# A graph layer's row gathers: GpSimd's gathers wait for the fetched rows, and for the sums eight groups back from group 8 on

## The reference

```python
h = maximum(layernorm(x), 0)
p1 = tanh(h @ pp_W1 + pp_b1) @ pp_W2 + pp_b2
inter = concatenate([p1[src], p1[dst]])          # per edge, 128 values
inter = ((inter @ pi_W1 + pi_b1) @ pi_W2 + pi_b2) @ pi_W3   # 64 x 8 per edge
i1 = einsum('ecb,eb->ec', inter, basis)
i1 = tanh(i1 @ ii_W1 + ii_b1) @ ii_W2 + ii_b2
out = x + segment_sum(i1, dst)
```

## Time and profile before

| | us |
|---|---|
| timed runs, median of 3 | 1991.06 |
| timed runs, lowest and highest | 1988.24, 1992.56 |
| profiled execution, its span | 2703.6 |
| TensorE matmuls busy in it | 1947.7 |
| VectorE busy | 1439.4 |
| ScalarE busy | 1089.0 |
| GpSimd busy | 1483.3 |

### The profile page before, as it was taken

One profiled execution on the slowest core, in us unless ns is written; L12 is line 12 of the kernel. 1 busy time (PEld: TensorE's weight loads), 2 busy tenths in 40 slices (PEclk: granted clock), 3 DMA queues, 4 the chain that ended last, 5 costly groups with the idle time before them and its releaser, 6 DMA issues.

```text
span 2703.6 us, 54970 instructions
## 1 busy us (share of the span) xinstructions
PE 1947.7 (72%) x20012; PEld 1270.4 (47%) x20012; DVE 1439.4 (53%) x1939; ACT 1089.0 (40%) x2419; POOL 1483.3 (55%) x1581
## 2 busy tenths in 40 slices
PE   4112987777777777777777777777777777787788
PEld 3101654444544544544445444455444444554556
DVE  4302875555555555555555555555555554555556
ACT  2211653434443343444444444444443343444344
POOL 4773025555655555665656566666655555555551
PEclk9555998888988888898988888988988788788889
DMA  4311222222221221222222222222222222222221
GB/s 86 80 28 31 58 46 43 44 45 42 50 49 39 48 47 41 51 50 43 50 46 45 49 49 45 49 48 45 50 46 45 44 46 43 44 44 42 42 42 45
DMA packets 261709, 127.00 MB, mean 47 GB/s; under 512 B 183561, under 2 KB 233720, under 8 KB 261448
## 3 DMA queue, kind: packets, MB, share of 16 engines
q1 hardware_dynamic: 209967, 74.11, 13.1%
q0 software_dynamic: 50048, 51.35, 10.4%
q10 hardware_dynamic: 1558, 0.15, 0.1%
HBM read 119.47 MB, written 6.00 MB: 46 GB/s over the span
## 4 chain that ended last, share of the span: by engine, by line
PE 66%; issue 19%; another core or an unknown queue 8%; ACT 5%; DVE 1%; DVEq 0%; ACTq 0%
PE bank L1337 34%; PE bank L1320 10%; PE bank L1344 7%; PE bank L1427 6%; PE spread_ps L1329 5%; PE bank L1304 3%; ACT tt_sb L702 2%; ACT st_sb L714 2%; PE bank L1352 0%; DVE o_sb L945 0%; PE spread_ps L1166 0%; ACT t_sb L705 0%; DVE acc_all L899 0%; DVE loc_bc L893 0%
## 5 line engine op out<-in xcount | busy, mean ns | idle before, releaser
L526 POOL DMA_INDIRECT u_rows<-u_tab,src_e x1436 | 1357.4, 945 | 1102.8 <-PE bank L1320 750.9
L1337 PE MATMUL bank<-o_sb,g_sb 128*64 128x256 f32 x6256 | 943.3, 453 | 153.2 <-issue 144.5
L945 DVE TENSOR_TENSOR o_sb<-st_sb,spread_ps 128x2048 f32<-128x2048 f32 x391 | 889.7, 2275 | 229.3 <-remote 111.3
L714 ACT ACTIVATE st_sb<-bank,s_bias 64x256 f32<-64x256 f32 x1564 | 733.1, 469 | 182.2 <-PE bank L1320 90.6
L1009 DVE TENSOR_TENSOR hot_t<-loc_bc,bank 126x512 bf16<-126x512 bf16 x391 | 268.4, 687 | 942.6 <-remote 615.3
L1337 PEld LDWEIGHTS bank<-o_sb,g_sb 128*64 128x64 f32 x6256 | 522.3, 162 | 434.7 <-issue 307.9
L702 ACT ACTIVATE tt_sb<-bank,z_bias 128x256 f32<-128x256 f32 x391 | 185.0, 473 | 706.1 <-PE bank L1337 364.4
L1344 PE MATMUL bank<-ident,tt_sb 128*128 128x128 f32 x782 | 183.3, 319 | 369.8 <-issue 211.1
L705 ACT COPY t_sb<-bank 128x256 f32<-128x256 f32 x391 | 146.1, 374 | 569.3 <-PE bank L1344 306.8
L1427 PEld LDWEIGHTS bank<-hot,t_sb 128*65 128x65 f32 x3128 | 224.4, 143 | 184.5 <-issue 182.1
L1427 PE MATMUL bank<-hot,t_sb 128*65 128x42 f32 x3128 | 274.5, 239 | 19.4 <-issue 18.6
(11 more groups left out here) (148 smaller groups left out, 361.9 us busy)
## 6 DMA issues: line engine op xcount, KB each, us to landing
loc_bc<-loc_tab SPq DMA_DIRECT2D x391, 126.0 KB
u_rows<-u_tab,src_e POOLq DMA_INDIRECT x1436
v_win<-v_tab SPq DMA_DIRECT2D x391, 15.8 KB
basis<-edge_attr SPq DMA_DIRECT2D x24, 256.0 KB
v_tab<-acc_all SPq DMA_DIRECT2D x6, 336.0 KB
basis<-u_tab,src_e POOLq DMA_INDIRECT x100
u_tab<-basis SPq DMA_DIRECT2D x6, 224.0 KB
x_sb<-x SPq DMA_DIRECT2D x1, 1120.0 KB
```

Of the source, the lines that this page charges most:

```text
L526: pool.indirect_dma_start(out=u_rows[:, g % UR, j, :] if g >= AHEAD else first_u[:, g - XG, j, :], out_offset=None, in_=u_tab[:, :], in_of ...
L714: last = nc.scalar.activation(tiles[h * D:(h + 1) * D, j], s_ps[part].rearrange("p (q a e) -> p q a e", q=2, a=TILES), ACT.Identity, bias= ...
L945: return nc.vector.tensor_tensor(o_sb[:, r, :, :].rearrange("p c (j e) -> p j c e", j=TILES), st_sb[:, r, :].rearrange("p (j e) -> p j e", ...
L1337: last = nc.tensor.matmul(z_ps[h * D:(h + 1) * D, 0:2 * P], g_sb[:, c, :], o_sb[:, r, c, 2 * h * P:(2 * h + 2) * P], start=(c == 0), stop= ...
```

## The change

It touches only the loop of GpSimd's gathers. One wait is added before it: the gathers of the u table start when the rows fetched from x have gone through tanh (`rows_tanh` at four). And the wait for the sums of group g-8, which stood from group 40 on, stands from group 8 on. Buffers, order, count and targets of the gathers stay.

```diff
@@ -514,13 +514,14 @@
             with pool.If(is_fast):
                 pool.wait_ge(u_stored, 32 * NC)
                 pool.wait_ge(ld[0], ld_count(0))
+                pool.wait_ge(rows_tanh, len(UNITS))
                 for g in range(XG, NG):
                     k = g // PIECE
                     if g == FULL:
                         pool.wait_ge(last_in, 32)
                     if g % PIECE == 0:
                         pool.wait_ge(ld[k % LD], ld_count(k))
-                    if g >= AHEAD + UR:
+                    if g >= UR:
                         pool.wait_ge(s_ready, g - UR + 1)
                     for j in range(TILES):
                         pool.indirect_dma_start(
```

## The result

The kernel after takes 2022.82 us (median of four runs, 2021.02 to 2023.33), the kernel before 1990.94 us. The ratio is 1.0153, with a 95% interval of 1.0141 to 1.0166: slower by 28 to 33 us. The prediction was 2018 us.

A forecast was written before the change was run, and what follows sets the result against it. GpSimd's issue of gathers was taken to bound the kernel from group 40 on. That group's start moves from T + 135 to T + 164, 29 us, less 1 us at the start: +27 us, 2018 us, range 1985 to 2032.

The forecast's parts named there:

- What bounds the kernel: GpSimd's issue of gathers sets the time from group 40 on, TensorE runs behind it; 68 + 1920 + 18 = 2006 us.
- The 18 us behind the last gather: End of the run: 16 us from the last group's transposes to the span's end, some 2 us for the landing.
- the delays of the start: Delays of 5 to 30 us early in the first profile, taken for a cost of recording and not counted on.
- The pace of 4.10 us: TensorE's own time per step, where no gathers run; claimed faster than GpSimd's 4.9 to 5.0 us per group.
- The sum: Group 40's start moves from T + 135 to T + 164 for any T over 97: 29 us, less 1 us; +27 us.
- T: End of the last tanh of the fetched rows, taken at about 100 to 125 us, upper bound 193.
- B: Time at which GpSimd begins group 40; before, the later of 232 us and T + 135; after, T + 164.
- The 3 us added for first steps not yet overlapped: An estimate within TensorE's time for group 32's sums in the kernel before: T + 1 + 32 x 4.10 + 3.
- Part (b): Group g waits for the sums of group g-8 from group 8 on, before from group 40; should cost nothing.
- part (a): The wait for rows_tanh at four before the first gather; gathers start at T, where before they began at 68.22.
- The rule on VectorE and GpSimd: GpSimd can't write gather descriptors during VectorE's two-port operations; by its ratio 132 gathers take some 820 us, not 164.
- The gathers' cost beside steps: What gathers add to TensorE's steps; bounds nothing or up to 2.3 us a step; at 0.7 the change costs 7 us.

The follow-up runs named there:

- the second look: The kernel before, unchanged, timed and profiled once more: ratio 1.001 (1.000 to 1.002), span 1991.4 us.
- (b) alone: The kernel before with only the wait for the sums of group g-8 moved to group 8 on, no wait for rows_tanh: 2017.15 us, ratio 1.0124.

## Why the prediction was right

**What bounds the kernel**: right, and from a profile in which GpSimd waited 750.9 us. The step that carried it was the sum that stands outside the profile's own pace: 1536 gathers x 1.25 us + 68 + 18 = 2006 us against 1991 measured. The distance of 1.25 us holds in normal runs (1.255 and 1.256 us on average from group 40 on), so the conclusion of "1.24 us or a little less" was slightly off. The 15 us over were not in the gathers, which take 9 us more than the 1920 of the sum, but in the start: the first u gather is at 42.72 in the second look and not at 68.22, 25.5 us earlier. The 18 us behind the last gather were 19.6 and 20.6 us; of the 2 us for the landing, the median measured is 2.8 us (2.3 to 4.7).

**That the delays of the start were not to be counted on**: right, shown by the second look at the kernel before. The reason given, a cost of recording, is only half supported: the second execution was profiled as well and has none of them. They belonged to that one execution; that recording as such makes them isn't borne out.

**The pace of 4.10 us**: right up to group 32. In the second look TensorE has group 32's sums by 204.6 us (their matmuls start at 203.89), 131.7 us after the first group's.

**The sum**: its size was right, the branch it took was not, and that its size was right is in part luck. I had T at 100 to 125 us and so let TensorE's group 32 set B before (T + 135). T, the end of the last tanh, is 71.5 us in the kernel after and 72.5 in the second look, below the 97 us from which that branch holds, and the start of the gathers lies at 42.72 and not at 68.22. The 3 us added for first steps not yet overlapped aren't seen either: TensorE has group 32's sums at T + 132, not T + 135. So GpSimd itself set B before, and the price is the plain difference of the first gathers: 72.28 - 42.72 = 29.6 us. B was 209.68 before and 238.46 after, 28.8 us apart, against the 29 predicted. Both branches gave the same number because TensorE has the sums of group 32 within 5 us of the time when GpSimd reaches group 40 (204.6 and 209.68). With T alone put right, the recorded sum would have given 232 against 72 + 164 = 236, a cost of 4 us. The two terms that were mis-sized, T by 30 to 50 us and the landing of u by 26 us, came from the first profile's late start, and their errors cancelled in the difference. The forecast of +27 us lies just under the measured 28 to 33. The two normal profiles are 27.8 us apart and the medians 31.9; no run here parts these 4 us from the scatter of single executions.

**Part (b) at no cost beside part (a)**: right; the kernel after waits 1.2 us in all for TensorE's sums (the line on L1321 in the fence below). Said of the pair, it hid that (b) alone would cost 26 us, which the prediction's own formula gives (T + 1 against the end of group 7's gathers).

**The rule on VectorE and GpSimd** of the page "SBUF — State Buffer" of the Trainium skill: the measurement decided against its price for this kernel. In the normal runs a gather takes a median 944 ns in the first hundred, nearly all of which lie beside VectorE's products in the kernel after, as the later ones do in the kernel before. The page's price is for two-port operations. The products here read one operand from SBUF and one from PSUM, and no run shows whether any VectorE operation in these steps is a two-port one, so the rule itself isn't tested. The summary lines of the kernel after and of the second look:

```profile
L527 POOL DMA_INDIRECT basis<-u_tab,src_e x100: 940/944/1453, 72.3 to 197.3; - x100
...
  PE bank L1321: 1.2, 4
```
```profile
L526 POOL DMA_INDIRECT basis<-u_tab,src_e x100: 940/944/1373, 42.7 to 167.8; - x100
```

**The gathers' cost beside steps**, left between nothing and 0.7 us a step: nothing that can be seen. TensorE runs 4.1 us steps in both kernels beside a full stream of gathers.

**Left open.** TensorE's first sums start at 72.18 us in the second look and at 71.00 in the kernel after, which fetches no rows of u by then. That may be the lighter DMA traffic at the start, but the kernels scatter by more: 68.7 to 72.2 us in those that gather from 41 to 43 us on, and 68.3 to 71.0 in those that wait for the tanh. No version that beats both came out of this: the kernel before has GpSimd gathering from 5 us to 1972 us with 4 us of stops, so fewer or cheaper gathers are what would bring it down (an argument, not a run), and no kernel here has fewer gathers and the whole result.

## What to carry to other kernels

When one queue's work, laid end to end, fills the run, the question to a new wait is only by how much it moves the first and the last item of that queue; several waits that hold it until the same moment cost once, not each. Lead that looks like idle stock (25 groups of buffers) is a head start for the slower engine, and its worth is read from which engine is slower, not from how long the queue waits. And a profile much longer than the timed runs may be used for durations and counts, but its waits and the time of its first events should be seen in a second profile before a term of a sum rests on them.

## What the runs showed of the hardware

The stream of gathers is very even: in the six profiles of normal runs with all four gathers the mean distance from group 40 to the end is 1.255 to 1.258 us. TensorE's granted clock is 1.00 in the window where it is busy 99% of the time and 0.94 in the one of the same length where it is busy 88% and waits for rows. 1.00 is the level of 2.4 GHz, the 0.50 of the earlier trace rows that of 1.2 GHz, and 0.94 a mean of both. Not expected was how far one execution can be off: the first profile of the kernel before had 2703.6 us, the second 1991.4 us, of the same instructions.
